# Layer 0: all the splitting of the mixture's weights in the two middle batches, two quarters in each

## The reference, cut to what matters

```python
x = L0_attn_x                                    # (4, 512, 256)
x = x + _L0_attn_ref(_layernorm(x), w_project, w_out)      # 16 heads of 16, causal softmax
x = x + _L0_ffn_ref(_layernorm(x), router_w, router_b, expert_w, expert_b)
#   logits = (h @ router_w.T + router_b) per output and expert; top 2 of 8 experts per output
#   final  = sum over experts of weight * (h @ expert_w.T + expert_b)
x = x + _L1_attn_ref(_layernorm(x), w_qkv, w_proj)
x = x + _L1_ffn_ref(_layernorm(x), gate, up, down)         # weights in a 4-bit format
```

## Time and profile before

| | |
|---|---|
| runs of the kernel | 1158.07, 1158.56, 1158.87 us; median 1158.56 us |
| the profiled execution | 1155.52 us |
| its span, first to last instruction | 1153.8 us |
| PE busy | 981.7 us, 85% of the span |
| DVE busy | 854.3 us, 74% |
| ACT busy | 498.0 us, 43% |
| POOL busy | 307.6 us, 27% |
| mean granted clock of PE | 0.941 of full speed |
| layer 0 attention in the trace | to about 280 us |

### The profile page before, as it was taken

The page is one execution under the profiler, slowest core; times in us unless marked ns, Lnnn a source line. Parts: engine busy times, 40 slices in busy tenths (PEclk is TensorE's granted clock), DMA queues, the critical chain, the costliest instruction groups (busy, mean ns, idle before and its releaser), DMA issues. The chain is left out here.

```text
span 1153.8 us, 19875 instructions
## 1 busy us (share of the span) xinstructions
PE 981.7 (85%) x6885; PEld 579.3 (50%) x6960; DVE 854.3 (74%) x1556; ACT 498.0 (43%) x972; POOL 307.6 (27%) x337
## 2 busy tenths in 40 slices
PE   3698989897789778797649799999978999999997
PEld 1444545454446344454214366575846555656564
DVE  5677776651999999999977875858762776777766
ACT  2154444453465464564624433416131444444443
POOL 3234343441352432423321121304044400000000
PEclk9799999998899989798769999999988999999999
DMA  6622222200101001001000010101011000000000
GB/s 176 118 75 77 72 82 67 74 2 4 44 0 47 1 1 45 0 1 46 1 17 3 10 30 8 31 2 32 8 36 39 20 1 19 1 18 0 19 1 19
DMA packets 37087, 35.87 MB, mean 31 GB/s; under 512 B 8584, under 2 KB 33416, under 8 KB 37008
## 3 DMA queue, kind: packets, MB, share of 16 engines
q1 hardware_dynamic: 35728, 33.79, 10.5%
q10 hardware_dynamic: 1280, 1.05, 0.7%
HBM read 27.28 MB, written 6.29 MB: 29 GB/s over the span
## 5 line engine op out<-in xcount | busy, mean ns | idle before, releaser
L883 DVE TENSOR_REDUCE bm<-ps 128x4 f32<-128x512 f32 x160 | 102.1, 684 | 32.6 <-PE ps L603 30.5
L782 ACT ACTIVATE pt<-ps 128x1024 f32<-128x1024 f32 (+1 forms) x96 | 82.0, 882 | 70.9 <-PE ps L679 70.2
L2011 ACT ACTIVATE g<-ps 128x512 f32<-128x512 f32 x64 | 38.2, 597 | 134.4 <-PE ps L1958 107.4
L2061 DVE SCALAR_TENSOR_TENSOR g<-g,ps 128x512 f32<-128x512 f32 x64 | 44.0, 687 | 54.7 <-ACT g L2011 54.5
L1753 DVE TENSOR_TENSOR qk_lo<-ps,qk_hi 128x512 bf16<-128x512 f32 x80 | 54.8, 686 | 40.1 <-ACT qk_hi L1646 34.1
L599 PE MATMUL ps<-ks,qs 96*128 96x512 bf16 (+3 forms) x256 | 68.7, 323 | 11.9 <-DMA ks<-scratch_k 7.6
L156 POOL TENSOR_TENSOR mag_w<-stage 128x512 f32<-128x512 fp8e4 x24 | 26.4, 1100 | 191.2 <-DVE stage L143 191.2
L1515 PE MATMUL ps<-wp_hi,oT_hi 128*128 128x256 bf16 x256 | 71.2, 278 | 5.4 <-DVE oT_lo L1746 5.4
L547 POOL TENSOR_SCALAR_AFFINE_SELECT pt<-pt 128x256 f32<-128x256 f32 (+1 forms) x96 | 45.9, 484 | 109.4 <-ACT pt L782 108.9
L1974 PE MATMUL ps<-ew_hi,it_hi 128*128 128x256 bf16 x256 | 69.8, 273 | 6.0 <-DVE it_lo L2077 6.0
L1646 ACT ACTIVATE qk_hi<-ps 128x512 bf16<-128x512 f32 x80 | 48.1, 603 | 55.0 <-PE ps L1515 55.0
(11 more groups left out here) (272 smaller groups left out, 2803.5 us busy)
## 6 DMA issues: line engine op xcount, KB each, us to landing
qs<-scratch_q SPq DMA_DIRECT2D x64, 64.0 KB, 2.6
ks<-scratch_k SPq DMA_DIRECT2D x48, 64.0 KB, 2.5
q_next<-in_w_qkv SPq DMA_DIRECT2D x4, 768.0 KB, 5.0
X<-in_x SPq DMA_DIRECT2D x4, 512.0 KB, 7.0
w_next<-in_router_w SPq DMA_DIRECT2D x4, 512.0 KB, 3.9
w_next<-in_expert_w SPq DMA_DIRECT2D x4, 512.0 KB, 4.7
p_next<-in_w_proj SPq DMA_DIRECT2D x4, 512.0 KB, 5.9
out<-X SPq DMA_DIRECT2D x8, 256.0 KB, 2.3
```

Of the source, the lines that this page charges most:

```text
L782: act.activation(pt[kt][:, heads[0]:heads[-1] + 1, :], src, ACT.Exp).then_inc(s_exp, 1)
L883: ins = dve.tensor_reduce(bm[:, 2 * g + i // 5, 4 * (i % 5):4 * (i % 5) + 4], src.rearrange("p (k q) -> p k q", k=4), AX_X, ALU.max)
```

## The change

The first and the last batch load and split nothing. Each middle batch b does two quarters, A = 2b - 2 and B = 2b - 1. POOL runs a piece behind every unit of g0 and g2 and behind u0 to u2 of g1 and g3, so nine pieces (one quarter) in g0 and g1 and nine in g2 and g3. SP loads quarter A at the start of the batch. Behind the last transfers of g1 it writes A's bias rows and then loads quarter B; behind those of g3 it writes B's bias rows. Some semaphores start from a value that makes the first waits pass, and PE's `first_router` waits once for all four quarters.

```diff
+                def load_quarter(q):
+                    sp.wait_ge(s_next, NEXT * (q + 1))
                     for n, name in enumerate(("router_w", "expert_w")):
-                        sp.dma_start(w_next[:, n, :, :], A[name].rearrange("(c p) (q n) -> q p c n", p=P, q=B)[b]
+                        sp.dma_start(w_next[:, n, :, :], A[name].rearrange("(c p) (q n) -> q p c n", p=P, q=B)[q]
                                      ).then_inc(load_next, 16)
...
+                def quarter_bias(q):
+                    wait_alone(sp, s_next, NEXT * (q + 2), passed_sp)
+                    for part in range(3):
+                        for m in range(2):
+                            sp.dma_start(b3_q[part:part + 1, q, m, :], b_part[m:m + 1, part, :]).then_inc(s_b3, 16)
+
+                def batch(b, first, last):
+
+                    if not first and not last:
+                        load_quarter(2 * b - 2)
...
                             stack_group(b + 1, g)
-
-                    wait_alone(sp, s_next, NEXT * b + NEXT, passed_sp)
-                    if first:
-                        wait_alone(sp, rows_set, E + 1, passed_sp)
-                    for part in range(3):
-                        for m in range(2):
-                            sp.dma_start(b3_q[part:part + 1, b, m, :], b_part[m:m + 1, part, :]).then_inc(s_b3, 16)
-
+                        if not first and not last and g % 2:
+                            quarter_bias(2 * b - 2 + g // 2)
+                            if g == 1:
+                                load_quarter(2 * b - 1)
+
+                wait_alone(sp, rows_set, E + 1, passed_sp)
+                sp.sem_inc(s_b3, 96)
                 all_batches(sp, batch)
-                sp.wait_ge(s_b3, 96 * B)
+                sp.wait_ge(s_b3, 96 * (B + 1))
...
             def _(pool):
+                pool.sem_inc(s_next, NEXT)
...
-                    more = work_between(split_next(b))
+                    more = work_between([] if first or last else split_next(2 * b - 2) + split_next(2 * b - 1))
...
-                            if last and g < 2 or g and u % 2:
+                            if g % 2 == 0 or u < 3:
                                 more()
...
-                    pe.wait_ge(s_next, NEXT * (B if u == NU - 1 else B - 1))
-                    pe.wait_ge(s_b3, 96 * (B if u == NU - 1 else B - 1))
+                    if u == 0:
+                        pe.wait_ge(s_next, NEXT * (B + 1))
+                        pe.wait_ge(s_b3, 96 * (B + 1))
```

More of the change, by code:

```diff
@@ L444, in _ @@
                 shift_group(0, 0, START.index(("turn", 0)))
-                def batch(b, first, last):
-                    reach(sp, s_next, NEXT * b)
+                def load_quarter(q):
+                    sp.wait_ge(s_next, NEXT * (q + 1))
                     for n, name in enumerate(("router_w", "expert_w")):
-                        sp.dma_start(w_next[:, n, :, :], A[name].rearrange("(c p) (q n) -> q p c n", p=P, q=B)[b]
+                        sp.dma_start(w_next[:, n, :, :], A[name].rearrange("(c p) (q n) -> q p c n", p=P, q=B)[q]
                                      ).then_inc(load_next, 16)
                     for n, name in enumerate(("router_b", "expert_b")):
-                        sp.dma_start(b_next[n:n + 1, :], A[name].rearrange("o (q n) -> q o n", q=B)[b]
+                        sp.dma_start(b_next[n:n + 1, :], A[name].rearrange("o (q n) -> q o n", q=B)[q]
                                      ).then_inc(load_b, 16)
+                def quarter_bias(q):
[6 more added lines that the diff above has]
+                        load_quarter(2 * b - 2)
                     for g, order, n, odd in schedule(b, first, last):
@@ L491, in piece @@
                             if n is not None:
-                                wait_alone(pool, s_next, NEXT * b + n, passed_pool)
+                                wait_alone(pool, s_next, NEXT * (b + 1) + n, passed_pool)
                             ins().then_inc(s_next, 1)
@@ L502, in first_bias @@
                         wait_alone(pool, load_b, 32 * b + 32, passed_pool)
-                        if not (isinstance(b, int) and b == 0):
-                            wait_alone(pool, s_b3, 96 * b, passed_pool)
+                        wait_alone(pool, s_b3, 96 * (b + 1), passed_pool)
                         pool.tensor_copy(b_part[:, 0, :], b_next[:, :]).then_inc(s_next, 1)
```

## The result

The changed kernel takes 1168.4 us (median of 6 runs, 1167.07 to 1170.68). The kernel before took 1158.51 us on the same chip (6 runs, 1156.31 to 1158.87). The ratio is 1.0096 with a 95% interval of 1.0083 to 1.011: slower. The medians lie 9.9 us apart (their quotient is 1.0085, inside the interval). The forecast was 1173 us and slower, 14.4 us above before.

A forecast was written before the change was run, and what follows sets the result against it. The prediction took PE to bound g1 to g3 and summed 21.2 - 4.4 - 0.85 (batch 0's g2) - 1.5 = +14.4 us onto the profiled 1155.52, giving 1169.9; the carried 3.0 us made it 1173 us, range 1167 to 1179.

The forecast's parts named there:

- What bounds the kernel, and quarter B: PE bounds g1 to g3; in middle batches' g2 the late load stalls PE 8.7 us, costing +10.6 us per batch.
- Quarter A and the bias pieces: In g0, g1 and g3 of middle batches: POOL's load wait and the bias pieces stay hidden from PE, counted 0.
- What lies inside the stretch: In g2 of middle batches: other delays from late POOL and SP, such as g2's `shift_group`, add nothing to the 10.6 us.
- Batch 3: No pieces left: PE's 2.86 us wait and 1.5 us of half-clock cost go, together -4.4 us.
- my bound of 4.6: The larger bound on batch 3's saving of 4.4 us; the smaller was 2.9.
- The start of batch 0: Without loads behind it `mt_lo` lands near 46.5; PE gains 1.1 us plus 0.4 us of half clock, -1.5 us.
- the lower bound, 0: At batch 0's start: the smallest saving allowed for `mt_lo`, against 1.5 us forecast and 4.0 us at most.
- The carried 3.0 us: The runs' median lay 3.0 us above before's profiled execution; added to 1169.9 to give 1173 us.
- (1): Slow clock reaches g3: 1.75 us more per middle batch, 1176.5; chance 0.23 shared with rival (2) and small savings.
- (2): Quarter B's load takes 6.7 us instead of 4.8: +1.9 us per batch, 1177; chance 0.23 shared with (1) and small savings.
- (3): In g2 the wait stays POOL's own, PE's being fully covered: 1152.7 us; chance of faster 0.04.
- (4): Stall in g2 is there but shorter, SP or load 2 us quicker: 4 us less, 1169; chance 0.09.

The follow-up runs named there:

- e1: Changed kernel with SP issuing quarter B's loads, then quarter A's bias rows, ahead of g1's `stack_group` transfers in middle batches; 1158.09 us, ratio 0.9992.
- e2: Changed kernel with only SP's order changed: quarter B's loads ahead of quarter A's six bias transfers, both still behind g1's transfers; 1162.52 us, ratio 1.0049.
- e3: Changed kernel with SP unchanged; POOL runs quarter B's pieces behind u5 of g2 and in g3; 1160.61 us, ratio 1.0039.
- e10: Changed kernel with e1's SP order and quarter B's pieces behind u1, u3, u5 of g2 and g3, four behind g3's u5; 1149.62 us, ratio 0.9939.
- e6: e3 with one SP step moved: g3's `mt` rows first, then bias rows and quarter B's loads, then g2's `stack_group`; 1165.48 us, ratio 1.0079.
- e9: Like e10 but g3's last pieces one behind u4, three behind u5; first `mt` rows ahead of the start's last `qs` transfers; 1146.69 us, ratio 0.9911.
- e8: The changed kernel run once more, unaltered, for its profile only; 1171.77 us.
- e11: e10's piece places and SP order combined with e9's start (first `mt` rows ahead of the last `qs` transfers); 1146.18 us, ratio 0.992.

## Why the prediction was right, and where it failed

**What bounds the kernel, and quarter B: right.** The forecast's central chain (bias rows ahead of the load, POOL's first piece waiting, the mask of u1 behind it, PE at `values` 0) is in the traces link by link. POOL's wait was 8.8 us for 9.0, PE's 8.3 for 8.7, issue to piece 4.9 for 4.8. From the first piece to g3 it was 227.33 - 217.69 = 9.64 us for 9.65. The cost was 10.31 and 10.40 us where 10.6 was forecast; the excess is SP's, which issued the load 4.9 us after `stack_group` and not 5.2. e1 and e2 show that the cause is the load's place on SP: 4.1 us earlier took 3.4 and 3.9 us off the stall, and the place ahead of `stack_group` took all of it. The forecast also set beside its 5.3 us for 1 MB a fit of the Trainium skill (DMA: Bandwidth & Descriptors, section on the anatomy of one DMA). That section gives the fit for transfers issued from GpSimd, one at a time; these are two, issued from SP, and the trace does not agree with the 4.4 us worked out from it: from the first issue to the piece it took 217.69 - 212.29 = 5.4 us.

**Quarter A and the bias pieces: right.** POOL waited for quarter A too, and PE didn't notice. POOL's timeline, g0 of batch 2 of the changed kernel:

```profile
179.22 1.04 POOL L509 CAST rw_hi<-w_next 128x1024 f32 x1 [6.43 <-DMA w_next<-in_expert_w]
```

g1 and g3 kept their lengths (9.50 and 9.44 us). g0 of batch 2 is 1.44 us longer, but by the windows its idle time is 3.36 us against 3.58 in the earlier trace rows; all of the difference is busy time at 0.88 of the clock instead of 0.94. In e1, with the same pieces in g0, it took 27.3 us.

**What lies inside the stretch: right by the sum, and with less cover than I wrote.** I said that the late `mt` rows of g3 cost nothing, since g3 starts late anyway. True for the changed kernel, but only because the mask's wait was longer. e3 took that wait away and met 3.44 us of the other. The forecast had not named that price.

**Batch 3: right, a little more.** PE went from 4.51 us idle to 1.81 and its busy time from 20.38 to 17.89 us; together 5.2 us, above my bound of 4.6. The clock was 1.00 in the whole of g0, where I had given back only the 3.5 us of the earlier trace rows at half price. The rest is a slow stretch of before that lies ahead of its wait, and that the forecast had not looked at. A window of PE alone in before's batch 3 shows it:

```profile
222.00:225.60 3.60, 3.60 (x20) 0.59 0.67 223
```

So this part is no effect of the wait, and such stretches come and go: without any piece in batch 3, g0 took 20.6 us in e2, e3 and e10 and 22.50 us in e6. PE's timeline of the changed kernel shows `values` 0 without a wait:

```profile
247.01 1.07 PE L703 MATMUL ps<-pt,v 128*32 128x512 f32 x8
```

**The start of batch 0: the step that failed.** "I take that `mt_lo` lands near 46.5 and PE gains 1.1 us" and 0.4 us more. PE gained nothing; it waited 2.51 us, and `mt_lo` took 5.6 us as before. PE's timeline, first score unit of the changed kernel:

```profile
48.02 0.59 PE L689 MATMUL ps<-qs,ks 98*128 98x512 bf16 x2 [2.51 <-DMA qs<-mt_lo]
```

I had seen in the earlier trace rows that `mt_hi` was as slow without a load close behind it, and still booked the difference between them to the loads. In these kernels the transfers behind don't delay it; those ahead do, as e9 shows. The true term was the lower bound, 0.

**The carried 3.0 us: failed in size.** The sum from the profiled execution gave 1169.9, against 1167.95 of the changed kernel's profiled one. I then added before's distance from execution to median. In the changed kernel that distance is 0.45 us. The time of this program differs by some 4 us between executions, and a distance seen once is not a property of the kernel. With the sum alone the forecast would have missed by 1.5 us instead of 4.6.

**How much of the sum is luck.** The sum of +14.4 us stands against +14.05 us in the traces. The chain in g2 earned that, but the smaller terms met it by cancelling: `mt_lo` came out 1.8 us worse than forecast and the two g0 2.2 us worse by the clock, while the stretch behind g0 of batch 3 (2.9 us) and batch 3 itself (0.8 us) came out better, both by the clock. e8, the same kernel, lost the 2.9 us again.

**The rivals.** (1) The clock reaching g3 didn't happen: g3 was 9.44 us. After each wait the clock was down, as windows of PE alone in g2 of batch 1 of the changed kernel show, and it was back before g3:

```profile
151.50:153.50 2.00, 2.00 (x14) 0.50 0.00 0
153.50:156.00 2.50, 2.50 (x21) 0.71 0.02 7
156.00:158.20 2.20, 1.59 (x24) 1.00 0.37 109
```

`values` 0 took 1.93 us instead of 1.07, and POOL still set the end of g2. (In before's batch 3, behind the wait of 2.86 us, `values` 0 itself still took 1.07 us, and the slow stretch came after it.) The Trainium skill (TensorE: Matmul & The Clock Gate, section on HAM oscillation) warns that each burst behind a long transfer wait starts throttled. The trace agrees with that, and here it cost nothing, since what ended the group was another engine's queue. In e3 it did cost: behind the wait of 3.44 us ahead of g3 no such queue covered the slow stretch, and PE's busy time in g3 grew by 1.7 us. (2) The load took 4.9 us, not 6.7; e6 shows that 7.1 can come, at another place. (3) The stall was not covered; PE has next to no work ahead of `values` 0 in g2. The 0.9 us in this rival's price come from no row; e1 shows that with the load in time the dense pieces cost 1.84 and 1.54 us in the two g2. (4) No shorter stall. The Trainium skill (DMA: Bandwidth & Descriptors, Rules for kernel authors) says to issue early and wait late. e1 agrees: for loads issued 6.1 and 5.8 us ahead of the piece POOL waited 0.26 us in batch 1 and not at all in batch 2, and g2 became 8.5 and 8.9 us shorter.

## What to carry to other kernels

When work that waits for a transfer is put in a helper engine's order, price three things: what stands ahead of the transfer on the queue that issues it, what stands behind the waiting piece on the helper, and who needs that next. When one wait is removed, look for the second that it had covered (3.4 us in e3, and one group on in e6) before the gain is written down. Keeping the first and last batch free of side work was worth 5 to 6 us here, but it showed in the time only once the load for the others was issued ahead of a long wait of the issuing queue.

## What the runs showed of the hardware

- **A small transfer's time went with what was ahead of it.** The 4 KB `mt` rows landed in 4.9 and 5.6 us behind the `qs` and `ks` transfers of the start, with 1 MB behind them (before) and without (the changed kernel). Over all kernels with those transfers ahead, `mt_lo` took 5.4 to 6.4 us. With four of them moved behind, the two rows took 3.3 and 3.9 us (e9), 3.7 and 4.2 us (e11).
- **The same 1 MB load took 4.7 to 5.6 us, and once each 6.1 and 7.1 us,** from the second issue to the first use, wherever POOL waited for it. The two long ones are those whose issue itself took 1.26 us (e1, batch 1) and 1.52 us (e6, batch 1) instead of 0.41 to 0.47.
- **Half-clock stretches fall differently at nearly the same waits.** The last projections took 3.69 us (4 traces) or 5.9 to 6.6 us (9 traces). g0 of batch 2 took 27.0 to 29.4 us at 1.00 to 0.88 of the clock, with 3.4 to 4.3 us of idle PE. g0 of batch 0 took 21.46 us at 1.00 (e9) to 24.75 us at 0.83 (e2). What sends them one way or the other is open. It makes a single profiled execution uncertain by some 4 us, and e1's runs by 7.
